# Softmax denominators by one selecting product and an in-place reciprocal, half of them inside the last head group, in a decoder block on one core

## The reference

```
# state-space layer: the steps
delta = softplus(dt_in @ dt_proj_w + dt_proj_b)      # = max(v, 0) + ln(1 + exp(-|v|))
# attention layer, 16 heads of width 16, in 4 groups of 4 heads
y = softmax(q k^T / 4, causal) v + softmax(cq ck^T / 4) cv
x = x + y @ Wp + bp
# expert layer: starts with layer norms of x, a gate product and top 2 of 8 experts
```

## Time and profile before

| | |
|---|---|
| time, median of 3 runs | 1751.97 us (1749.2 to 1752.84) |
| the profiled execution | 1748.14 us, span 1746.4 us |
| PE busy | 84% of the span |
| DVE busy | 74% |
| ACT busy | 47% |
| POOL busy | 37% |
| mean granted TensorE clock | 0.937 |

### The profile page before, as it was taken

One profiled execution on the slowest core, in us unless ns is written; L12 is line 12 of the kernel. 1 busy time (PEld: TensorE's weight loads), 2 busy tenths in 40 slices (PEclk: granted clock), 3 DMA queues, 4 the chain that ended last, 5 costly groups with the idle time before them and its releaser, 6 DMA issues. The chain is left out here.

```text
span 1746.4 us, 19466 instructions
## 1 busy us (share of the span) xinstructions
PE 1465.1 (84%) x6552; PEld 728.4 (42%) x6552; DVE 1284.1 (74%) x1979; ACT 816.5 (47%) x1582; POOL 648.2 (37%) x630
## 2 busy tenths in 40 slices
PE   5697879997997799988988899866588998599895
PEld 2353522243554232254543232422242224388784
DVE  5999588868996878769986888689958872344424
ACT  3643436756453266755434467553342674222121
POOL 2565431313864412208643232157543131222220
PEclk9899979998999899989998899989997999699998
DMA  4960452003002522021005420210044202257744
GB/s 119 335 189 1 118 134 59 15 13 138 16 1 61 147 70 47 14 97 57 0 21 138 94 60 27 80 61 6 1 118 109 60 14 87 75 190 239 236 133 145
DMA packets 128069, 153.87 MB, mean 88 GB/s; under 512 B 19110, under 2 KB 107695, under 8 KB 125921
## 3 DMA queue, kind: packets, MB, share of 16 engines
q1 hardware_dynamic: 124224, 143.96, 28.3%
q0 software_dynamic: 3744, 8.66, 1.4%
HBM read 102.82 MB, written 50.99 MB: 88 GB/s over the span
## 5 line engine op out<-in xcount | busy, mean ns | idle before, releaser
L172 PE MATMUL PS<-arena 128*32 128x512 f32 (+10 forms) x4150 | 826.3, 448 | 66.4 <-DVE maxs L1916 20.5
L172 PEld LDWEIGHTS PS<-arena 128*32 128x32 f32 (+3 forms) x4150 | 363.0, 128 | 508.6 <-ACT arena L1884 186.7
L1884 ACT ACTIVATE arena<-PS 128x512 f32<-128x512 f32 (+3 forms) x768 | 362.1, 552 | 255.7 <-PE PS L172 252.3
L1438 POOL TENSOR_TENSOR arena<-arena 128x1024 f32<-128x1024 f32 x124 | 292.6, 2361 | 200.6 <-DVE arena L1461 107.4
L1912 DVE TENSOR_REDUCE maxs<-PS 128x1 f32<-128x1024 f32 x256 | 297.7, 1214 | 42.6 <-PE PS L172 42.5
L1461 DVE TENSOR_TENSOR_SCAN arena<-PS,arena 128x1024 f32<-128x1024 f32 x128 | 292.0, 2282 | 0.7 <-ACT PS L1410 0.7
L172 PE MATMUL PS<-arena,ident 128*128 128x512 f32 (+1 forms) x560 | 247.1, 565 | 5.4 <-DVE arena L1470 5.4
L1410 ACT ACTIVATE PS<-arena,A_neg 128x511 f32<-128x511 f32 x256 | 165.9, 681 | 183.0 <-DVE arena L1461 179.2
L1609 POOL TENSOR_SCALAR_AFFINE_SELECT arena<-arena 128x128 f32<-128x128 f32 x256 | 73.0, 298 | 255.7 <-ACT arena L1884 251.0
L1470 DVE TENSOR_TENSOR arena<-arena,PS 128x1024 f32<-128x1024 f32 x128 | 156.2, 1220 | 6.9 <-PE PS L172 2.8
L172 PEld LDWEIGHTS PS<-arena,ident 128*128 128x128 f32 x560 | 105.0, 192 | 88.0 <-issue 71.3
(11 more groups left out here) (275 smaller groups left out, 1548.6 us busy)
## 6 DMA issues: line engine op xcount, KB each, us to landing
arena<-in_ew SPq DMA_DIRECT2D x46, 512.0 KB, 4.8
arena<-stack_parts SPq DMA_DIRECT2D x288, 64.0 KB, 2.3
rows_in<-nil SPq DMA_DIRECT2D x16, 1088.0 KB, 12.6
arena<-b_rows SPq DMA_DIRECT2D x16, 1024.0 KB, 8.0
stack_parts<-arena SPq DMA_DIRECT2D x40, 384.0 KB, 2.8
arena<-stack_parts SPq DMA_DIRECT2D x96, 128.0 KB, 4.2
arena<-rows_in SPq DMA_DIRECT2D x23, 272.0 KB, 5.1
xn<-dens SPq DMA_DIRECT2D x24, 256.0 KB
```

Of the source, the lines that this page charges most:

```text
L172: return nc.tensor.matmul(o, l, r, start=start, stop=stop)
L1438: nc.gpsimd.tensor_tensor(b_sb[i % 2], u[:, 2 * kh:2 * kh + 2, :], Brow[:, n, :].unsqueeze(1).to_broadcast([P, 2, T]), ALU.mult).then_inc( ...
L1884: nc.scalar.activation(probs[(HG * s + h) % NPR][:, 0:N], ring_bank(n)[:, 0:N], ACT.Exp, scale=HD ** -0.5).then_inc(S["ring_read"], 1)
```

## The change

Four parts.

1. **Turning is replaced by selecting.** `turned_sums`, `spread_sums`, the small reciprocal and the widening copy go. One product of `den_sel` with the 128x512 half of `YS` puts each denominator on all 32 rows of its head, in PSUM; DVE inverts that whole 128x512 tile in place and multiplies from it.
2. **The causal half moves into the last group.** `causal_sums` stands at step 5 of the last group, after two of its scores and ahead of the next sequence's input products (bank 3); `causal_heads` (reciprocal and product) stands on DVE ahead of the four copies and convolutions. The second channel tile's products wait until bank 3 is free again (`den_ready`).
3. **The order of the changeover.** PE projects groups 0 to 2 of all four token tiles while DVE inverts the context half, then adds group 3; `steps_in` comes after the projection. DVE does `residual`, `norms` and `columns` before `split`. Each token tile has a bank of its own (5, 6, 7 and 4 or 0).
4. **The positive part.** In the three changeovers that begin a sequence, ACT forms max(v + bias, 0) with a Relu from banks 1 to 4 between Exp and Ln; DVE's `steps_of_time` stays for the first sequence only. The gate products, which overwrite banks 1 to 3, wait for it (`abs_done`).

```
-        turned_sums(): 8 products; spread_sums(): 8 products
+                def context_sums():
+                    pe.wait_ge(S["pv_copied"], 2 * NG)
+                    if begins:
+                        pe.wait_ge(S["xp_ready"], DT)
+                    mm(bank(2), den_sel[:], YS[(NG - 1) % 2][0], True, True).then_inc(S["turned_mm"], 1)
+
+                def project(t, groups):
+                    for g in groups:
+                        pe.wait_ge(S["y_ready"] if g < NG - 1 else S["den_ready"], g + 1 if g < NG - 1 else NG + 1)
+                        last = mm(bank(ROW_BANKS[t])[:, 0:DM], YT[g][:, tok(t)], wp[:, g, :], g == 0, g == NG - 1)
+                    if g == NG - 1:
                         last.then_inc(S["wp_mm"], 1)
...
                 if ends:
                     pe.wait_ge(S["ring_read"], HG * STEPS * NG)
-                    turned_sums()
+                    project(0, range(2))
+                    context_sums()
+                    project(0, range(2, NG - 1))
+                    for t in range(1, TT):
+                        project(t, range(NG - 1))
+                    for t in range(TT):
+                        project(t, (NG - 1,))
...
                     if ends:
                         pe.wait_ge(S["abel_pre"], TT)
+                        pe.wait_ge(S["abs_done"], 2 * DT)
...
                 elif begins:
-                    spread_sums()
                     steps_in()
-                    project()
...
                     link(ins)
+                    if ends:
+                        for m in range(DT):
+                            nc.scalar.activation(delta[:, m, :], bank(1 + m), ACT.Relu, bias=dt_b[:, m:m + 1])\
+                                .then_inc(S["abs_done"], 1)
                     for m in range(DT):
                         nc.scalar.activation(tmp[:, m, :], tmp[:, m, :], ACT.Ln, bias=1.0).then_inc(S["sp_ready"], 1)
...
                 def last_heads():
+                    y = YS[(NG - 1) % 2]
                     dve.wait_ge(S["turned_mm"], 2)
...
+                    fed(nc.vector.reciprocal(bank(2), bank(2)))
+                    fed(nc.vector.tensor_tensor(y[0], y[0], bank(2), ALU.mult))
+                    dve.wait_ge(S["den_ready"], NG)
+                    nc.vector.tensor_tensor(YT[NG - 1], y[0], y[1], ALU.add).then_inc(S["den_ready"], 1)
...
                 if ends:
-                    last_sums()
                     last_heads()
-                if begins:
-                    split()
-                if ends:
                     residual()
                     norms()
                     columns()
                 if begins:
+                    split()
+                if begins and not ends:
                     steps_of_time()
...
+                def causal_sums():
+                    pe.wait_ge(S["pv_copied"], 2 * NG - 1)
+                    if b + 1 < NB:
+                        pe.wait_ge(S["xT_ready"], 4)
+                    mm(bank(3), den_sel[:], YS[(NG - 1) % 2][1], True, True).then_inc(S["turned_mm"], 1)
...
+                        if k == 0 and m == 1:
+                            pe.wait_ge(S["den_ready"], NG)
...
+                        if g == NG - 1 and k == SPREAD_AT:
+                            causal_sums()
...
+                def causal_heads():
+                    y = YS[(NG - 1) % 2][1]
+                    dve.wait_ge(S["turned_mm"], 1)
+                    link(nc.vector.reciprocal(bank(3), bank(3)))
+                    nc.vector.tensor_tensor(y, y, bank(3), ALU.mult).then_inc(S["den_ready"], 1)
```

More of the change, by code:

```diff
@@ L130, in decoder @@
         den_c = sb("den_c", [2 * HG * TT, P])
-        den_t = sb("den_t", [P, 2 * TT * HG])
-        den_wide = xn[:].rearrange("p (i a) n -> p i (a n)", i=2)
         m8 = sb("m8", [P, TT, 8])
@@ L793, in entry @@
             begins, ends = b < NB, b >= 1
+            ROW_BANKS = (5, 6, 7, 4 if begins else 0)
             GATE_BANKS = (7, 1, 2, 3) if ends else (1, 2, 3, 4)
@@ L850, in tensor @@
             def tensor(pe):
-                def turned_sums():
+                def context_sums():
                     pe.wait_ge(S["pv_copied"], 2 * NG)
[L853 to L874, removed]
+                    if begins:
[6 more added lines that the diff above has]
+                    if g == NG - 1:
                         last.then_inc(S["wp_mm"], 1)
@@ L976, in tensor @@
                             pe.wait_ge(S["z_ready"], m + 1)
+                        elif m == DT - 1:
+                            pe.wait_ge(S["res_read"], TT)
                         mm(bank(1 + m), dt_w[:, m * P:(m + 1) * P], dtin[:], True, True).then_inc(S["dt_mm"], 1)
@@ L1088, in residual @@
                         dve.wait_ge(S["wp_mm"], t + 1)
-                        o = bank(5 + t % 3)[:, (t // 3) * DM:(t // 3 + 1) * DM]
-                        nc.vector.tensor_tensor(x1[:, t, :], x1[:, t, :], o, ALU.add).then_inc(S["res_read"], 1)
+                        nc.vector.tensor_tensor(x1[:, t, :], x1[:, t, :], bank(ROW_BANKS[t])[:, 0:DM], ALU.add).then_inc(S["res_read"], 1)
                         dve.wait_ge(S["res_read"], t + 1)
@@ L1238, in vector @@
                 if begins:
+                    split()
+                if begins and not ends:
                     steps_of_time()
-                    if not ends:
-                        nc.vector.memset(PS[:, 0:4, 0:1], 0.0).then_inc(S["dve_chain2"], 1)
+                    nc.vector.memset(PS[:, 0:4, 0:1], 0.0).then_inc(S["dve_chain2"], 1)
                 if ends:
@@ L1492, in attend @@
             HEADS_IN = 16 * 2 * 6
-            COLUMNS_AT = TT
+            COLUMNS_AT, SPREAD_AT = TT, TT + 1
             NEXT_AT = {5: (0, 1), 6: (2, 3), 7: (4,), 8: (5,), 9: (6,), 10: (7,)}
@@ L1977, in vector @@
                         nc.vector.tensor_copy(xT[:, k, :], bank(2 + k)).then_inc(S["xT_ready"], 1)
+                    causal_heads()
                     for m in range(DT):
```

## The result

| | before | changed |
|---|---|---|
| time, median of 4 runs each, in turn on one chip | 1750.59 us | 1723.52 us (1720.78 to 1725.45) |
| ratio, 95% interval | | 0.9847 [0.9827, 0.9866] |
| the profiled execution's span | 1746.4 us | 1719.1 us |
| mean granted TensorE clock | 0.937 | 0.945 |

The change makes the kernel 27 us faster; 33 was forecast, 1718.9 us.

The account below looks back on a forecast made before the run. The prediction took serial changeovers as the bound, with handovers between PE, DVE and ACT on the path and no engine full. Three changeovers' 25.0 plus the last one's 8.1 gave 33.1; 1751.97 - 33.1 = 1718.9 us, range 1706 to 1733.

Parts of the forecast that it names:

- R: DVE's reciprocal of a 128x512 tile: 3.24 us, at 6.0 ns an element; bounds 0.69 and 5.7.
- D: Rival, slower: the in-place reciprocal with source and target in PSUM costs about 8 us; chance 0.05.
- C: Rival: the reciprocal is dearer than its slope by x, costing 7x; 1726.6 us at x = 1.1; chance 0.13.
- The group: Last attention group: 1.45 us longer, 0.9 in the last sequence; the second tile's product waits 0.3 to 0.4.
- this sign of being wrong: In the last group: the prediction is wrong if ring steps past step 6 stay stretched.
- The path: Changeover, from the start of the last values: residual at 8.2 us, transposes 17.4, last logits pass 25.3, decays 38.5.
- The clock: In the changeover the granted clock stays at 1.00 through `abel`, which takes 3.6 us instead of 5.84.
- B: Rival: the clock falls all the same, `abel` takes 5.84 us, 6.7 in three changeovers, 1725.6; chance 0.20.
- The three changeovers: Last values to first decay: 39.95 us against 48.75 and 48.02; gains 8.8, 8.1 and 8.1, together 25.0.
- The last changeover: Changeover ahead of the expert work: 20.2 us to the transposes against 28.3, a gain of 8.1.
- F: Rival: a reciprocal of 0.69 us saves 2.55 at each context half, 11.4 in all, 1707.5; chance 0.05.
- E: Rival: moving the positive part does not move the changeover's end, ACT becomes last; 1722.7 us; chance 0.07.

Follow-up runs that it names:

- part 4 alone: The kernel before with the Relu and the gates' wait added and `steps_of_time` taken from the changeovers, nothing else: 1753.41 us, 1.0014.
- six extra products: Six unread 128x512 products among the last changeover's bias products, added to the kernel with turning kept, split spread and ten idle products: 1727.84 us, 0.9876.
- reordered kernel: The changed kernel with parts 1 and 2 undone (turning kept), PE's new order and the Relu kept: 1723.06 us, 0.9849.

## Why the prediction was right, and where its sizes were off

The mechanism held: a serial changeover, shortened on PE's and DVE's path. The gain was 27.1 and not 33.1; the time looks closer, 1723.5 against 1718.9, because the forecast started from 1751.97 and the kernel before took 1750.59 beside the changed one. The terms, in the order of the working:

- **R.** 3.24 predicted from the two small forms, 3.37 measured, source and target in PSUM: 3.37 - 0.933 over 384 elements is 6.3 ns each. D falls with it, and C, whose price began at 1.1 above. The estimate by the Trainium skill (VectorE: DVE Perf Modes, "First, the fixed hardware budget"), 4.3 us for a repeat count of 8, does not fit the 3.37.
- **The group.** 1.45 and 0.9 predicted; 1.69, 1.69, 2.04 and 1.2 measured. The second tile's wait is there, 0.49 against 0.3 to 0.4. Past step 6 the shift no longer grows (1.69 at the product at 363.37, 1.68 at the last values), so this sign of being wrong did not appear. Together 1.4 us short over the four, of which 0.35 in the third comes and goes between executions (23.38 in two kernels that leave the group as it was).
- **The path.** Predicted and measured, from the start v of the last values: reciprocal's start v + 3.0 / 3.0; PE's cover ends v + 7.4 / 7.3; residual v + 8.2 / 8.6; `steps_in` ends v + 13.05 / 13.3; transposes v + 17.4 / 17.6; Relu ends v + 24.7 / 24.2; last logits pass ends v + 25.3 / 25.5; decays v + 38.5 / 38.9. Each link held within 0.5. The `split` took 3.77 (396.43 to 400.20), 3.6 predicted.
- **The clock.** 1.00 through `abel`, as forecast, in all three changeovers; B is out in the changed kernel. The price was real: in the nine changeovers with PE idle 2.7 to 2.8 us ahead of the transposes (three each in the kernel before, with PE's order undone, and with part 4 alone) `abel` took 5.54 to 6.48. B itself, a fall without such a wait, was seen once, in the third changeover with part 2 undone. So the argument against B, that the idle stretch goes, doesn't exclude it.
- **The three changeovers.** 25.0 predicted, 22.2 by the ledger. Of the 2.8, 1.1 is the group and 0.44 in each is the path; the last 0.4 is in the third, which had no rows of its own in the prediction.
- **The last changeover.** 8.1 predicted, 8.1 measured, in part by luck: to the transposes it was 20.7 with the group's 1.2, where 20.2 was summed (19.54 from 1440.22 to 1459.76), so 7.5 were gained there, and 0.6 came behind them.
- **Outside the sum:** the first expert tile, 1.4 us longer, and the other untouched stretches, 1.5 longer. I had let the expert work "start that much earlier" at its old length. Other kernels with the new order and no idle products ran this tile in 6.93 to 8.49 us against 7.08 before, and the untouched stretches together scatter by up to 7 between kernels, so neither is shown to be the change's. They make up 2.9 of the 6 that are missing from the gain.
- **F.** I gave a cheap context reciprocal 2.55 a changeover "if all arms follow". With a copy the stretch fell by 0.85: PE's own projections are right behind. The sum itself had said so (cover to v + 7.4, DVE ready at v + 7.7), and F's price contradicts it. The inversion is nearly covered; a dearer one would not have been.
- **E.** No extra load appears (1.28 once, after the Relu), the Relu passes end before the logits do, and ahead of the decays ACT waits 1.34 us for DVE. Undoing the Relu passes costs 9.1, where 8 were summed.

What I did not see is which part earns the gain. The parts don't add. PE's order alone is worth 16.8 us with the others in place. The Relu is worth 9.1 with the new order, nothing in the old one. The selecting product with the in-group half, the parts that the change is named for, is worth nothing beside the turning it replaces, once turning runs in the new order: 1723.13 against 1723.06. With a selecting product for both halves behind the group it is 14.6 worse: given part 1, part 2 is needed, since it pays for the second reciprocal of 3.37 us. In the old PE order they, with DVE's new order and the Relu, still bring 10 us (1739.92); which of them does was not run apart, and DVE's new order was never undone by itself. That the turning loses more there because nothing covers it is my reading, not shown.

For the passes themselves the Trainium skill (ScalarE: Activation LUTs, "Rules for kernel authors") would leave the positive part on VectorE. Measured, four passes take 2.42 us on ACT and 2.73 on DVE, and the 9.1 and the zero above show that the place in the order decides, not the engine's rate.

## What to carry to other kernels

In a serial stretch, first look for work that can stand beside the slow step: a projection of the parts already finished covered a 3.37 us reciprocal and also kept PE from idling. Price a removed step as it would run in the new order, not as its row shows it in the old one: at full clock the two turning steps took 0.63 and 0.54 of what their rows said. Move passes to another engine only where the trace says that the first one ends last, and test each part in both surroundings.

## What the runs showed of the hardware

- A PE wait can cost twice. After idle times of 2.75, 2.76, 3.73 and 4.11 us the granted clock was at 0.50; after those of up to 1.21 us in the changed kernel's three full changeovers it was still 1.00. It isn't a rule either way: after 3.98 us one product still ran at full clock (1.16), and the clock fell without a long wait in the third changeover with part 2 undone and in the bias products of the last changeover, where with the six extra products it stayed at 0.50 for 20 us of unbroken work.
- The clock was also 0.50 in the first expert tile, after a wait of 11.89 us for rows. With ten products of no use in front the tile's products took 5.19, 3.69 and 3.69 us in three kernels, and 5.18 to 6.73 in the ten without. Put ahead of work that was not waiting, such products cost 10.8.
- Small f32 products follow the clock: 16 of 128x128 took 3.64 us in the earlier trace rows and 1.95 in the reordered kernel.
- A DVE pass between SBUF tiles can last as long as POOL's instruction beside it: the first cast of the split took 1.12 and 1.28 us while POOL had a tile pass under way, its twin at 398.30 took 0.42, and so did both in the kernel before, where POOL had nothing to do. By the Trainium skill (SBUF — State Buffer, "SBUF: two separate sides") DVE and GpSimd share a port pair under an exclusive lock, and the cast's end at 398.27, 0.3 us after that of POOL's pass (397.98), agrees.
- Identical executions differ by up to 2.7 us in single attention stretches; below that, only the marker stretches of the first three changeovers, which repeat to 0.2, can be compared.
